# Attention scores as float16 products of 64-row strips, with the strips written on GpSimd

## What is computed

```python
h = concatenate([cls, patches @ W_lin.T + b_lin])          # 197 x 192 per image
x = _layernorm(h)
q, k, v = split(x @ qkv_weight.T)                          # 12 heads of 16
q = _layer_norm(q) * SCALE                                 # over the 16 of a head
k = _layer_norm(k)
attn = softmax(einsum('bhnd,bhmd->bhnm', q, k))
h = h + (attn @ v) @ proj_weight.T
h = h + mixture_of_experts(_layernorm(h))                  # 8 experts, top 2, and a shared one
```

## Time and profile before

| What | Value |
|---|---|
| Median of 3 runs (lowest, highest) | 1763.53 us (1762.55, 1765.28) |
| Profiled execution: time, span | 1764.9 us, 1763.0 us |
| Busy over the span: TensorE, VectorE, ScalarE, GpSimd | 96%, 73%, 56%, 19% |
| Busy from 400 to 500 us: TensorE, VectorE, ScalarE, GpSimd | 98.74, 68.91, 63.40, 3.69 us |
| Granted TensorE clock, mean | 0.984 of full speed; 1.00 from 100 us to the end of phase A's full steps |

### The profile page before, as it was taken

The page is one execution under the profiler, slowest core; times in us unless marked ns, Lnnn a source line. Parts: engine busy times, 40 slices in busy tenths (PEclk is TensorE's granted clock), DMA queues, the critical chain, the costliest instruction groups (busy, mean ns, idle before and its releaser), DMA issues. The chain is left out here.

```text
span 1763.0 us, 45476 instructions
## 1 busy us (share of the span) xinstructions
PE 1695.0 (96%) x17682; PEld 1180.2 (67%) x17682; DVE 1290.8 (73%) x3660; ACT 984.6 (56%) x2088; POOL 336.7 (19%) x402
## 2 busy tenths in 40 slices
PE   4999999999999999999999599999999999999998
PEld 4777777777777777777777345555555555555555
DVE  4677776666666666666666278888888888888887
ACT  2666666666666666666666354454545454545453
POOL 1000000000000000000000033434343434344433
PEclk8999999999999999999999799999999999999999
DMA  7233333333333333333320101010101010101000
GB/s 230 66 74 74 74 75 74 74 74 70 70 72 74 73 73 73 74 75 74 74 54 12 42 10 37 20 37 19 37 20 37 19 37 19 37 19 37 16 19 16
DMA packets 40866, 95.26 MB, mean 54 GB/s; under 512 B 4491, under 2 KB 17454, under 8 KB 40526
## 3 DMA queue, kind: packets, MB, share of 16 engines
q1 hardware_dynamic: 31438, 72.89, 13.2%
q0 software_dynamic: 9216, 19.47, 7.3%
HBM read 92.44 MB, written 19.37 MB: 63 GB/s over the span
## 5 line engine op out<-in xcount | busy, mean ns | idle before, releaser
L1309 POOL TENSOR_TENSOR in_lo<-inner,in_hi 128x512 f16<-128x512 f32 (+1 forms) x225 | 257.7, 1145 | 433.7 <-ACT act L1096 433.7
L575 ACT ACTIVATE prob<-ps_sc 99x792 f32<-99x792 f32 x384 | 310.7, 827 | 53.1 <-PE ps_sc L390 53.1
L1242 DVE SCALAR_TENSOR_TENSOR acc<-ps_y,comb,acc 128x192 f32<-128x192 f32 (+1 forms) x700 | 241.9, 407 | 0.3 <-PE ps_y L1038 0.3
L1104 ACT ACTIVATE in_hi<-inner 128x512 f16<-128x512 f32 (+1 forms) x225 | 140.3, 623 | 181.3 <-DVE inner L1224 181.3
L1096 ACT ACTIVATE act<-ps_h 128x512 f32<-128x512 f32 (+1 forms) x225 | 131.8, 586 | 189.7 <-PE ps_h L1022 189.7
L1224 DVE SCALAR_TENSOR_TENSOR inner<-ps_h,act 128x512 f32<-128x512 f32 (+1 forms) x225 | 153.7, 683 | 103.4 <-ACT act L1096 99.8
L1036 PE MATMUL ps_y<-w_hi,in_hi 128*128 128x192 f16 (+1 forms) x900 | 224.1, 249 | 4.1 <-DVE acc L1242 1.9
L1038 PE MATMUL ps_y<-w_hi,in_lo 128*128 128x192 f16 (+1 forms) x900 | 221.6, 246 | 0.0
L1037 PE MATMUL ps_y<-w_lo,in_hi 128*128 128x192 f16 (+1 forms) x900 | 221.5, 246 | 0.0
L331 PE MATMUL ps_hid<-lin_hi,x_hi 128*99 128x192 f16 x768 | 192.7, 251 | 21.3 <-DVE x_lo L685 10.6
L844 POOL DMA_DIRECT2D x_hi<-xp x64 | 34.0, 532 | 869.5 <-PE ps_hid L333 868.7
(11 more groups left out here) (154 smaller groups left out, 3670.5 us busy)
## 6 DMA issues: line engine op xcount, KB each, us to landing
xin<-xp SPq DMA_DIRECT2D x64, 594.0 KB, 4.3
x_hi<-xp POOLq DMA_DIRECT2D x64, 297.0 KB, 4.0
hidden_dram<-h SPq DMA_DIRECT2D x64, 147.0 KB
hin<-hidden_dram SPq DMA_DIRECT2D x24, 384.0 KB, 3.1
out<-acc SPq DMA_DIRECT2D x24, 384.0 KB, 2.3
w_f<-w SPq DMA_DIRECT2D x1, 2304.0 KB, 8.9
hidden_dram<-h SPq DMA_DIRECT2D x64, 0.8 KB
w_f<-w SPq DMA_DIRECT2D x1, 864.0 KB, 10.8
```

What stands on the lines that cost most here:

```text
L575: act.activation(prob[quad][:, places].rearrange("p h m s -> p h (m s)"), ps_sc[0:TR, places, 0:2 * SLOTS], ACT.Exp, scale=D ** -0.5 / (SQ ...
L1242: last = dve.scalar_tensor_tensor(out=acc[p][0:R, t, :], in0=ps_y[half_no][0:R, u * C:(u + 1) * C], scalar=comb[p][0:R, t, e:e + 1], in1=b ...
L1309: pool.tensor_tensor(in_lo[b][:, 0:N], inner[b][:, 0:N], in_hi[b][:, 0:N], ALU.subtract).then_inc(inlo_done, 1)
```

## The change

- `qk_norm[t]` keeps only 16 columns a head. GpSimd has a new `strips_of(n, t)`: a copy (L880 of the new file) that writes each normalised head rounded to float16 twice, next to each other, and a subtraction (L882) that writes the remainder (the float32 value less its float16 rounding). Both go into `qk_strips[t]`, where a head has a strip of 64 columns: low, high, high, zeros for q, and high, high, low, zeros for k. So one product over 48 rows is low*high + high*high + high*low.
- `transpose_qk` takes six float16 chunks of 128 columns (two heads each) in place of three float32 ones, by a float16 identity `id16` that ScalarE makes once, and waits for `qklo_done` of GpSimd in place of `qknorm_done` of VectorE. `qkT_ps` holds six chunks of float16 (pitch 100), so `qT_copy` and `kT_copy` move 594 float16 numbers a row in place of 297 float32 ones.
- `scores` does the same eight matmuls of 198 columns a quad, in float16, two heads side by side in the array (rows 0 to 63 and 64 to 127) in place of four.
- `qk_normalise` waits for GpSimd's read of the buffer one image earlier. GpSimd's loop issues the load of image k and then writes the strips of image k-3.

```diff
--- before.py
+++ after.py
@@ -35,7 +35,9 @@
 PAIRS = HEADS // 2
 QUAD = 4
 QUADS = HEADS // QUAD
-QB = 32
+HS = 64
+CHUNKS = HEADS // 2
+KSHIFT = D
 VB = 32
 EXPERTS, INTER = 8, 128
 NE = EXPERTS + 1
@@ -163,9 +165,11 @@
             qk_var = sa("qk_var", [TR, 2 * HEADS])
             qk_lnvar = sa("qk_lnvar", [TR, 2 * HEADS])
             qk_rstd = sa("qk_rstd", [TR, 2 * HEADS])
-            qk_norm = [sa(f"qk_norm{t}", [TR, 2 * HEADS, QB]) for t in range(2)]
-            qT = [sa(f"qT{p}", [128, QUADS, SLOTS]) for p in range(2)]
-            kT = [sa(f"kT{p}", [128, QUADS, SLOTS]) for p in range(2)]
+            qk_norm = [sa(f"qk_norm{t}", [TR, 2 * HEADS, D]) for t in range(2)]
+            qk_strips = [sa(f"qk_strips{t}", [TR, 2, HEADS * HS + 3 * KSHIFT], F16) for t in range(2)]
+            id16 = sa("id16", [128, 128], F16)
+            qT = [sa(f"qT{p}", [128, CHUNKS, SLOTS], F16) for p in range(2)]
+            kT = [sa(f"kT{p}", [128, CHUNKS, SLOTS], F16) for p in range(2)]
             v = [sa(f"v{p}", [TR, 2, HEADS, VB]) for p in range(2)]
             prob = [sa(f"prob{q}", [TR, QUAD, 2, SLOTS]) for q in range(QUADS)]
             oT = [sa(f"oT{p}", [128, QUADS, SLOTS]) for p in range(2)]
...
@@ -210,7 +214,13 @@
         hid = ps_hid[0:TR, 0:2 * C].rearrange("p (t c) -> p t c", t=2)
         x_feat = ps_qk[:, 0:2 * SLOTS].rearrange("p (k s) -> p k s", k=2)
         qk_ps = ps_qk[0:TR, 0:2 * C].rearrange("p (h d) -> p h d", d=D)
-        qkT_ps = ps_mix[:, 0:QUADS * TR].rearrange("p (b s) -> p b s", s=TR)
+        qkT_ps = ps_mix[:, 0:CHUNKS * (TR + 1) // 2].bitcast(F16).rearrange("p (b s) -> p b s", s=TR + 1)[:, :, 0:TR]
+        KFIRST = HEADS * HS + KSHIFT
+        flat = [x[:].rearrange("p b e -> p (b e)") for x in qk_strips]
+        strips = [x[:, D:D + 2 * HEADS * HS].rearrange("p (h e) -> p h e", e=HS) for x in flat]
+        high_twice = [x[:, :, 0:2 * D].rearrange("p h (two d) -> p h two d", two=2) for x in strips]
+        high_once = [x[:, :, 0:D].rearrange("p (b h) d -> p b h d", b=2) for x in strips]
+        low_once = [x[:, :, 0:HEADS * HS].rearrange("p b (h e) -> p b h e", e=HS)[:, :, :, 0:D] for x in qk_strips]
         o_feat = ps_mix[:, 0:2 * SLOTS].rearrange("p (k s) -> p k s", k=2)
         o_tok = ps_mix[0:TR, 0:QUADS * 128].rearrange("p (h e) -> p h e", e=VB)
         tok = ps_mix[0:TR, 0:2 * C].rearrange("p (t c) -> p t c", t=2)
@@ -243,6 +253,7 @@
         h_done, stats_done, mv_done = sem("h_done"), sem("stats_done"), sem("mv_done")
         xnorm_done, xTlo_done, qkvar_done, qknorm_done = (
             sem("xnorm_done"), sem("xTlo_done"), sem("qkvar_done"), sem("qknorm_done"))
+        qkhi_done, qklo_done, id16_set = sem("qkhi_done"), sem("qklo_done"), sem("id16_set")
         rden_done, onorm_done, onTlo_done, h2_done = (
             sem("rden_done"), sem("onorm_done"), sem("onTlo_done"), sem("h2_done"))
 
@@ -367,13 +378,15 @@
             def transpose_qk(n, t, w):
 
                 if w == 0:
-                    pe.wait_ge(qknorm_done, n.times(2, t + 1))
+                    if n.c == 0 and t == 0:
+                        pe.wait_ge(id16_set, 1)
+                    pe.wait_ge(qklo_done, n.times(2, t + 1))
 
                 if reached(n.times(4, 2 * t + w)):
                     pe.wait_ge(qkT_out, n.times(4, 2 * t + w))
-                part = qk_norm[t][:, w * HEADS:(w + 1) * HEADS, :].rearrange("p (b h) e -> p b (h e)", h=QUAD)
-                for b in range(QUADS):
-                    last = pe.transpose(qkT_ps[:, b, :], part[:, b, :], id32[0:TR, 0:TR])
+                for b in range(CHUNKS):
+                    last = pe.transpose(qkT_ps[:, b, :], flat[t][:, w * KFIRST + b * 128:w * KFIRST + b * 128 + 128],
+                                        id16[0:TR, 0:TR])
                 last.then_inc(qkT_done, 1)
 
             def scores(n, quad):
@@ -386,9 +399,10 @@
                     pe.wait_ge(exp_done, n.times(PAIRS, 2 * quad))
                 for m in range(2):
                     for place in range(QUAD):
-                        rows = slice(QB * place, QB * place + QB)
-                        last = pe.matmul(sc[:, place, m, :], kT[p][rows, quad, m * TR:(m + 1) * TR],
-                                         qT[p][rows, quad, :], start=True, stop=True)
+                        rows = slice(HS * (place % 2), HS * (place % 2) + HS)
+                        chunk = 2 * quad + place // 2
+                        last = pe.matmul(sc[:, place, m, :], kT[p][rows, chunk, m * TR:(m + 1) * TR],
+                                         qT[p][rows, chunk, :], start=True, stop=True)
                 last.then_inc(sc_done, 1)
 
             def attend(n, quad):
@@ -622,6 +636,8 @@
                     mixture_piece(k.c - FIRST_PIECE)
 
             attention_weights()
+            act.wait_ge(consts_a_loaded, 16 * len(consts_a))
+            act.activation(id16[:], id32[:], ACT.Copy).then_inc(id16_set, 1)
             act.wait_ge(consts_set, 1)
             run(step)
 
@@ -730,9 +746,9 @@
             def qk_normalise(n, t):
                 dve.wait_ge(qkrstd_done, n.times(2, t + 1))
 
-                if reached(n.times(4, 2 * t - 2)):
-                    dve.wait_ge(qkT_done, n.times(4, 2 * t - 2))
-                dve.tensor_tensor(qk_norm[t][:, :, 0:D], qk_ps,
+                if reached(n.times(2, t - 1)):
+                    dve.wait_ge(qklo_done, n.times(2, t - 1))
+                dve.tensor_tensor(qk_norm[t][:], qk_ps,
                                   qk_rstd[:].unsqueeze(2).broadcast_to([TR, 2 * HEADS, D]),
                                   ALU.mult).then_inc(qknorm_done, 1)
 
@@ -849,15 +865,28 @@
             pool.memset(minus_half[:], -0.5)
             pool.memset(eps_qk[:], (SS / SQ) ** 2 * EPS)
             for t in range(2):
-                pool.memset(qk_norm[t][:], 0.0)
+                pool.memset(qk_strips[t][:], 0.0)
             for p in range(2):
                 pool.memset(v[p][:], 0.0).then_inc(v_zeroed, 1)
             pool.wait_ge(v_zeroed, 2)
             for p in range(2):
                 last = pool.memset(v[p][:].rearrange("p t h e -> p (t h) e")[:, :, D:D + 1], 1.0)
             last.then_inc(consts_set, 1)
-            for k in range(3, IMAGES):
-                load_first(Index(0, k))
+            def strips_of(n, t):
+                pool.wait_ge(qknorm_done, n.times(2, t + 1))
+
+                if reached(n.times(4, 2 * t - 2)):
+                    pool.wait_ge(qkT_done, n.times(4, 2 * t - 2))
+                pool.tensor_copy(high_twice[t], qk_norm[t][:].unsqueeze(2).broadcast_to([TR, 2 * HEADS, 2, D])).then_inc(qkhi_done, 1)
+                pool.wait_ge(qkhi_done, n.times(2, t + 1))
+                pool.tensor_tensor(low_once[t], qk_norm[t][:].rearrange("p (b h) d -> p b h d", b=2), high_once[t],
+                                  ALU.subtract).then_inc(qklo_done, 1)
+
+            for k in range(3, IMAGES + 3):
+                if k < IMAGES:
+                    load_first(Index(0, k))
+                strips_of(Index(0, k - 3), 0)
+                strips_of(Index(0, k - 3), 1)
 
 
 def phase_b(nc, hidden_dram, out, sem, sb, bufs):
```

More of the change, by code:

```diff
@@ L194, in phase_a @@
      h, stats, meanvar, h_rstd, h_lnvar, xnorm, xT_hi, xT_lo, qk_sq, qk_var, qk_lnvar, qk_rstd,
-     qk_norm, qT, kT, v, prob, oT, o_rden, o_norm, onT_hi, onT_lo, h2) = (
+     qk_norm, qk_strips, id16, qT, kT, v, prob, oT, o_rden, o_norm, onT_hi, onT_lo, h2) = (
         bufs[n] for n in (
@@ L198, in phase_a @@
             "h stats meanvar h_rstd h_lnvar xnorm xT_hi xT_lo qk_sq qk_var qk_lnvar qk_rstd "
-            "qk_norm qT kT v prob oT o_rden o_norm onT_hi onT_lo h2").split())
+            "qk_norm qk_strips id16 qT kT v prob oT o_rden o_norm onT_hi onT_lo h2").split())
     with ExitStack() as ctx:
```

## The result

The changed kernel takes **1769.28 us** (median of 6 runs, 1768.42 to 1769.84), the kernel before beside it 1762.38 (1761.21 to 1765.28): ratio 1.0037, 95% interval 1.0024 to 1.0050. It is slower, by 0.4%, a little more than the 0.2% that this measurement can't tell from no change. The profiled execution took 1769.26 us, span 1767.5, granted clock 0.984.

What follows compares the result with a forecast made beforehand. Each step was taken as bound by a ring of waits through TensorE, VectorE and ScalarE, not by TensorE alone. +0.09 us times 61 steps is +5.5, with the end +4.3: 1769.2 profiled, forecast 1767.8 us, range 1758 to 1799.

Steps and rivals of the forecast that it cites:

- The ring: One step as three parts: TensorE alone 5.03 us, VectorE with ScalarE 8.53, TensorE 1.26; sum 14.82.
- Scores at I and N: Two of TensorE's three score quads, in the part VectorE and ScalarE set: 0.4 us gained each, worth nothing.
- TensorE is the bound: Rival: TensorE's work sets the time, so a step gains 1.19 us, giving 1690 us; chance 0.05.
- q copy: ScalarE's copy of 594 numbers takes 0.664 us, counts twice a step, and starts TensorE's piece G 0.11 us later.
- T: TensorE's piece after the S scores, waiting for ScalarE's copy of q: starts 0.02 us earlier, not 0.4.
- k copy: VectorE's copy of 594 float16 numbers out of PSUM takes 0.47 us, two numbers a cycle, so nothing moves.
- The rival at 0.78: VectorE's copy of k runs at the float32 rate, 0.78 us: +0.55 us a step, 1796 us; chance 0.15.
- Transposes: Six float16 transposes on TensorE take 0.26 us in place of three float32 ones in 0.25: +0.01 us.
- The end: Last image, whose scores no other image hides: quads save about 0.5 us each, exposed copy costs 0.24; -1.2 us.
- GpSimd: Copy and subtraction take 2.0 us a half, 4.0 of a 14.82 us step, hidden within 5.9 and 6.0 us.
- the cover ends at three times my cost: GpSimd's work per half, taken as 2.0 us, would stay hidden up to three times that.
- The rival that said this: GpSimd at 2.6 us a half overlaps VectorE's xnorm: 0.2 to 1 us a step, 1776 to 1825 us; chance 0.08.

Runs made afterwards that it cites:

- run 1: Changed kernel with the eight score matmuls of quad 1 done twice on TensorE: 1770.30 us, ratio 1.0053 to the kernel before.
- run 2: Changed kernel with six of TensorE's float16 transposes per step done twice: 1787.63 us, ratio 1.0147 to the kernel before.
- run 5: Changed kernel with VectorE's four xnorm instructions moved behind v_copy and ScalarE's second square put before h_rstds: 1730.49 us, ratio 0.9815 to the kernel before.
- run 6: Kernel before with xnorm moved behind v_copy on VectorE and ScalarE's second square put before h_rstds: 1745.94 us, ratio 0.9905.
- run 8: Changed kernel with GpSimd's copy and subtraction done twice for each half: 1830.09 us, ratio 1.0385 to the kernel before.
- run 10: Changed kernel with GpSimd's copy and subtraction done twice for half 0 alone: 1831.19 us, ratio 1.0397 to the kernel before.
- late xnorm: VectorE's xnorm moved behind v_copy, ScalarE's second square earlier; alone in the kernel before 1745.94 us, with float16 scores and q copied in words 1707.43 us.
- the short copy: Changed kernel with ScalarE copying q as 300 words of 32 bits in place of 594 float16 numbers: 1746.37 us, ratio 0.9916 to the kernel before.
- the kernel with the second half doubled: Changed kernel with GpSimd's copy and subtraction done twice for half 1 alone: 1771.63 us, ratio 1.0061 to the kernel before.

## Why the prediction was right

- **The forecast**, 1767.8 us, is 1.5 us under the median, well inside the range, and the sign is right. Of the change itself, +4.3 us was forecast, and +6.9 measured between the medians. The profiled executions agree better, 1769.2 forecast and 1769.26 measured, and some of that is luck. The one before stood 2.5 us over the median of its six runs, the one after at its own. And terms made up for each other: the step in the middle grew by more than forecast and the first images took 0.65 us where I had put nothing, but ten of the steps that I had counted didn't grow at all.
- **The ring** holds (runs 1, 2, 5 and 6). Scores at I and N were worth nothing; adding to N was free, adding at C was paid in full. The rival "TensorE is the bound", 1690 us, is refuted.
- **q copy**: 0.664 forecast, 0.668 measured; G +0.09 for +0.11.
- **T** is the term of the step that was mis-sized: forecast 0.02 us earlier after R, measured 0.04 later (1.30 for 1.26). I took 0.06 us from the copy's end to TensorE, from the o_norm row; here it is 517.54 - (516.72 + 0.68) = 0.14, while the copy began 0.04 us sooner after R than I had it. With G's +0.09 and -0.02 from G to R the step is +0.11 and not +0.09.
- **k copy**: 0.47 forecast, 0.472 measured. The rival at 0.78, to which I gave 0.15, is gone. The Trainium skill (Vector Engine (DVE) Microarchitecture Reference, 5.1 Performance modes) had two elements a cycle for it, and this trace agrees: 594 float16 numbers take as long as 297 float32 ones.
- **Transposes**: six in 0.27 us (E at 506.54 to F at 506.81), 0.26 forecast.
- **The end** gave back 1.2 us, as forecast.
- **GpSimd**: 1.81 us a half for 2.0, hidden as forecast. But "**the cover ends at three times my cost**" was wrong, shown by runs 8 and 10. I measured the cover by who waits for the strips (5.9 us) and not by whom the work stands beside. It ends when GpSimd is still at work at xnorm, 0.46 us later than now. With 1.7 us more for half 0 that cost 0.86 us a step, 62 us in all; how the cost rises between the two no run shows. The rival that said this had the place right (xnorm, "0.2 to 1 us a step") and got a chance of 0.08; its point, 2.6 us a half, was near too (1.81 + 0.46 = 2.27), and the text contradicts itself by not using it for the bound.

## What to carry to other kernels

Cut the step at the waits into a ring and ask of each saving in which part it lies: 54 us off TensorE's busy time bought nothing, while 0.25 us off a copy that two parts wait for bought 23 us, and four short instructions moved to a later place on VectorE, with one on ScalarE, bought 39. When work moves to an idle engine, check not only who needs its result but which instructions of the other engines will stand beside it. A change that looks worthless can be the half of a pair: late xnorm alone gives 0.9%, together with the float16 scores and the short copy 3.1%.

## What the runs showed of the hardware

- **GpSimd and VectorE hold each other up, in both directions.** Beside GpSimd's row VectorE's float32 tensor_scalar from SBUF to SBUF (xnorm) takes 0.54 us for 0.38 and 1.01 for 0.31, its float16 copy in SBUF 0.90 for 0.18, and w_lo, an operation with two inputs in SBUF, 0.67 for 0.41. With x_lo, which has two inputs in SBUF as well, it is GpSimd that is stretched (0.91 to 1.87 us, and the copy 0.82 to 1.80 in the kernel with the second half doubled), while x_lo stays at 0.77. VectorE's rows that read PSUM (v, 0.56 us) are as long beside GpSimd as without it. The Trainium skill (SBUF — State Buffer, Who interferes with whom) names these kinds of VectorE instruction, and the trace agrees. It also says that whoever issues first gets the shared ports and the other waits. By the recorded starts that fits the first xnorm row and w_lo, but not x_lo (GpSimd's row began 0.33 us earlier) nor the second xnorm row (it began 0.04 us before GpSimd's). Recorded spans of GpSimd are rough, so what decides is not shown here.
- **ScalarE copies float16 by the number, not by the byte**: 594 numbers 0.668 us, the same bytes as 300 float32 words 0.42 us. VectorE takes 0.47 us for 594 float16 or 297 float32 numbers.
- **Two 64-row float16 products run beside each other**: eight of 198 columns in 0.39 to 0.48 us, where one after the other at the 0.43 ns a column of F would be 0.68.
